# A two-layer AdaLN and FFN kernel: W_dec by two queues and six of eight pieces on VectorE, table rows gathered into W1T's memory, the last FFN's scale and offset on ScalarE, and a new order of steps

## The reference

```
U = (cond_512 @ W_dec + b_dec).reshape(B, 129, 30)      # one matrix for each of 128 sequences
x = x @ (U[:, :-1] @ V) + U[:, -1] @ V                  # layer 0, condition
gate = x @ Wg.T + bg; the two best of 8 experts, softmax of the two
x = x + sum over the two: w * (gelu(x @ W1[e].T + b1[e]) @ W2[e].T + b2[e])
h = ln(ln(x, pw[id], ...), cp[c], ...); t = ln(x, tm[c], ...); s = ln(x, ms[m], ...)
m, n, r = x + three small MLPs of the condition         # rows of the tables by token
x' = ln(silu(concat(w0*h, w1*t, w2*m, w3*n, w4*r, w5*s) @ int_W1 + b) @ int_W2 + b2, int_g, int_be)
f = silu(x' @ w1) * (x' @ w2); f = gelu(f @ h1); f = gelu(f @ h2); x = x + f @ w3    # scaled ternary weights
```

## Time and profile before

| | us |
|---|---|
| median of 3 runs | 456.68 |
| lowest and highest | 456.17, 460.87 |
| the profiled execution | 454.07 |
| its span | 452.2 |

### The profile page before, as it was taken

The page is one execution under the profiler, slowest core; times in us unless marked ns, Lnnn a source line. Parts: engine busy times, 40 slices in busy tenths (PEclk is TensorE's granted clock), DMA queues, the critical chain, the costliest instruction groups (busy, mean ns, idle before and its releaser), DMA issues.

```text
span 452.2 us, 5963 instructions
## 1 busy us (share of the span) xinstructions
PE 425.7 (94%) x1897; PEld 283.9 (63%) x1897; DVE 328.6 (73%) x693; ACT 278.7 (62%) x498; POOL 141.2 (31%) x135
## 2 busy tenths in 40 slices
...
GB/s 235 386 250 93 112 125 256 67 79 204 134 120 144 8 87 227 110 46 13 167 46 46 96 230 6 8 151 166 33 46 77 137 0 2 0 0 25 0 1 50
DMA packets 16847, 45.06 MB, mean 100 GB/s; under 512 B 3209, under 2 KB 5166, under 8 KB 16238
## 3 DMA queue, kind: packets, MB, share of 16 engines
...
...
## 4 chain that ended last, share of the span: by engine, by line
PE 68%; DVE 5%; ACT 4%; issue 2%; POOL 1%; POOLq 0%; ACTq 0%; DVEq 0%
PE bank L737 20%; PE bank L635 18%; PE bank L683 6%; PE bank L777 5%; PE bank L627 5%; PE bank L722 5%; PE bank L690 2%; PE bank L651 2%; PE bank L766 1%; POOL rstd L1421 1%; DVE bn L1163 1%; DVE mG L1153 1%; PE bank L678 1%; PE bank L696 1%; PE bank L646 1%
## 5 line engine op out<-in xcount | busy, mean ns | idle before, releaser
L635 PE MATMUL bank<-mG,W 128*128 128x512 f32 x256 | 120.8, 599 | 0.5 <-DVE mG L1153 0.5
L882 ACT ACTIVATE mG<-bank,keepP 128x512 f32<-128x512 f32 x128 | 85.9, 683 | 33.7 <-PE bank L627 27.0
L1421 POOL TENSOR_TENSOR rstd<-ve,mhalf 128x4 f32<-128x4 f32 x24 | 34.4, 1434 | 177.9 <-DVE ve L1169 177.1
L1153 DVE TENSOR_TENSOR mG<-mG,gwbs 128x1024 f32<-128x1024 f32 x64 | 78.9, 1240 | 1.9 <-DMA gwbs<-gate_w 1.6
L635 PEld LDWEIGHTS bank<-mG,W 128*128 128x128 f32 x256 | 47.5, 192 | 41.3 <-issue 36.8
L627 PE MATMUL bank<-ts,A 96*128 96x512 f32 x128 | 63.8, 533 | 6.8 <-ACT mG L882 5.0
L943 ACT ACTIVATE G<-bank,keepP 128x512 f32<-128x512 f32 x48 | 32.6, 690 | 26.1 <-PE bank L737 25.9
L1401 POOL DMA_INDIRECT gp<-pgb_in,ixall x32 | 39.9, 1247 | 22.4 <-DVE w_l L1069 11.6
L627 PEld LDWEIGHTS bank<-ts,A 96*128 96x128 f32 x128 | 24.0, 191 | 26.7 <-issue 12.6
L737 PE MATMUL bank<-hA_h,h1w_h 128*128 128x512 f32 x96 | 38.8, 404 | 0.0
L737 PE MATMUL bank<-hB_h,h2w_h 128*128 128x512 f32 x96 | 38.8, 404 | 0.0
...
## 6 DMA issues: line engine op xcount, KB each, us to landing
...
W1T<-W1T_in SPq DMA_DIRECT2D x1, 1024.0 KB, 10.0
...
```

The source lines that it names most:

```text
L635: mm = pe.matmul(OACC[:, :], W2[:, e * HC + c, :], mG[n % NMG][:, c, :], start=False, stop=(e == E - 1 and c == HC - 1))
L882: act.activation(mG[e % NMG][:, c % HC, :], HM[n % 2][:, :], ACT.Gelu, bias=b1c[:, c:c + 1]).then_inc(m_gelu, 1)
L1153: dve.tensor_tensor(mG[n % NMG][:, :, :], mG[n % NMG][:, :, :], gwb[(n // 2) % 2][:, n % 2, :].unsqueeze(1).broadcast_to([P, HC, T]), ALU. ...
L1421: step(pool.tensor_tensor(rstd[:, n, :], ve[:, n, :], mhalf[:, :], ALU.pow))
```

## The change

- W_dec comes by two DMAs, rows 0 to 31 from SyncE's queue and 32 to 63 from ScalarE's, ahead of cond_512 and b_dec there. ScalarE issues all its loads before it waits for W_dec, and runs one small activation (`warmA`) that loads its table.
- `PIECES` gives VectorE six pieces of W_dec and ScalarE two (the fourth and the sixth). `WARM` is 5 instead of 6. The products of U still have 65 rows.
- `gap` is 512 columns longer and `ct` lies behind `norms`, so `gp0` lies in W1T's memory and `gap`'s, and the wait for `small_src` goes.
- The splits of the last FFN's weights come in the order h2, w3, h1, w12 instead of w3, w12, h1, h2.
- `ff` is an activation on ScalarE instead of a VectorE instruction.
- The whole `ORDER` is new.

```diff
-        gap = sb("gap", [P, 6144 - KR * (D + 1) - E * H], stack=early)
+        gap = sb("gap", [P, 6656 - KR * (D + 1) - E * H], stack=early)
...
-        WARM = 6
+        WARM = 5
+        PIECES = ("v", "v", "v", "a", "v", "a", "v", "v")
...
             "POOL": (
-                (0, "ix tcl0 tcl1 tcl2 tcl3 srt tcl4 tcl5 tab tcl6 rt0 tcl7 rt1"),
+                (0, "tcl0 tcl1 tcl2 srt tcl3 tcl4 tcl5 ix tab rt0 tcl6 rt1 tcl7"),
...
-            load(Wd[0:MU, :], A["W_dec"], ld_wd)
+            load(Wd[0:MU // 2, :], A["W_dec"][0:MU // 2, :], ld_wd)
...
+            def ff(b):
+                act.wait_ge(yT_mm, b + 1)
+                act.activation(flat(YN), XL[:, :], ACT.Identity, scale=igb[:, 0:1], bias=igb[:, 1:2]).then_inc(f_full, 1)
...
+            load(Wd[MU // 2:MU, :], A["W_dec"][MU // 2:MU, :], ld_wd)
             load(muT[0:MU, :], A["cond_512T"], ld_wd)
             load(Wd[MU:MU + 1, :], A["b_dec"], ld_wd)
+            load(Vk[:, :], A["V"], ld_v)
             load(keepP[:, :], A["keepP"], ld_v)
-            load(Vk[:, :], A["V"], ld_v)
-            act.wait_ge(setup0, 1)
-            act.wait_ge(ld_wd, 48)
             load(earlyP[:, :], A["earlyP"], ld_small)
-            wd = Wd[0:MU + 1, :].rearrange("m (i k) -> m k i", k=KR)
-            for q in range(1, 8, 2):
-                act.activation(Wp[:, 4 * q:min(4 * q + 4, KR), :], wd[:, 4 * q:min(4 * q + 4, KR), :], ACT.Copy).then_inc(wd_odd, 1)
             for b in (1, 2):
                 load(keep[b][:, :], A["xT"][:, b * T:(b + 1) * T], x_in[b])
             load(xTr[0][:, :], A["xT"][:, 3 * T:5 * T], ld_x[0])
             load(w12s[:, :], A["w12T"], ld_w[0])
+            act.wait_ge(setup0, 1)
+            act.activation(warmA[:, :], onesf[:, :], ACT.Copy)
+            act.wait_ge(ld_wd, 64)
+            wd = Wd[0:MU + 1, :].rearrange("m (i k) -> m k i", k=KR)
+            for q in range(8):
+                if PIECES[q] == "a":
+                    mine = slice(4 * q, min(4 * q + 4, KR))
+                    act.activation(Wp[0:MU + 1, mine, :], wd[:, mine, :], ACT.Copy).then_inc(wd_act, 1)
...
-            def ff(b):
-                dve.wait_ge(yT_mm, b + 1)
-                dve.tensor_scalar(flat(YN), XL[:, :], igb[:, 0:1], igb[:, 1:2], ALU.mult, ALU.add).then_inc(f_full, 1)
...
-            dve.wait_ge(ld_wd, 48)
-            for q in range(0, 8, 2):
-                dve.tensor_copy(Wp[:, 4 * q:4 * q + 4, :], wd[:, 4 * q:4 * q + 4, :]).then_inc(wd_even, 1)
+            dve.wait_ge(ld_wd, 64)
+            for q in range(8):
+                if PIECES[q] == "v":
+                    mine = slice(4 * q, min(4 * q + 4, KR))
+                    dve.tensor_copy(Wp[0:MU + 1, mine, :], wd[:, mine, :]).then_inc(wd_dve, 1)
...
-                    pool.wait_ge(small_src, NSMALL)
```

More of the change, by code:

```diff
@@ L137, in build @@
         sa, syT = sz, sth
-        muT = sb("muT", [MU + 1, B], stack=early)
+        muT = sb("muT", [P, B], stack=early)
         Vk = sb("Vk", [KR, P], stack=early)
@@ L160, in build @@
         h1s, h2s = parts(hs, 2048, 2048)
-        Wp = hs[0:MU + 1, 0:KR * (D + 1)].rearrange("m (k i) -> m k i", k=KR)
+        Wp = hs[:, 0:KR * (D + 1)].rearrange("m (k i) -> m k i", k=KR)
+        warmA = sb("warmA", [2, P], stack=early)
         keepB = sb("keepB", [P, 2 * E], stack=early)
@@ L190, in build @@
         xh, tt, ss, hh = [norms[:, i, :, :] for i in range(4)]
-        cs_, ch = [sb(f"c{k}", [P, T]) for k in "sh"]
+        ct, cs_, ch = [sb(f"c{k}", [P, T]) for k in "tsh"]
         TH = sb("TH", [P, T])
@@ L295, in weights_done @@
         def weights_done(eng, *ns):
-            eng.wait_ge(w_lo, max((1, 2, 3, 4)[n] for n in ns))
+            eng.wait_ge(w_lo, max((4, 3, 1, 2)[n] for n in ns))
         def wide(v, n):
@@ L806, in _ @@
             for k in range(KR):
-                if k % 8 == 0:
-                    pe.wait_ge(wd_even, k // 8 + 1)
-                elif k % 8 == 4:
-                    pe.wait_ge(wd_odd, k // 8 + 1)
+                if k % 4 == 0:
+                    who = PIECES[k // 4]
+                    pe.wait_ge(wd_dve if who == "v" else wd_act, PIECES[:k // 4 + 1].count(who))
                 if k == 28:
                     pe.wait_ge(vt_ready, 1)
-                    pe.matmul(bank[7][0:KR, 256:256 + B], Wp[:, :, D], muT[:, :], start=True, stop=True)
+                    pe.matmul(bank[7][0:KR, 256:256 + B], Wp[0:MU + 1, :, D], muT[0:MU + 1, :], start=True, stop=True)
                     pe.wait_ge(ld_small, 16)
@@ L818, in _ @@
                     pe.transpose(bank[7][:, 384:384 + KR], Vk[:, :], ident[0:KR, 0:KR]).then_inc(vt_mm, 1)
-                mm = pe.matmul(bank[k // 4][:, (k % 4) * B:(k % 4 + 1) * B], Wp[:, k, 0:D], muT[:, :], start=True, stop=True)
+                mm = pe.matmul(bank[k // 4][:, (k % 4) * B:(k % 4 + 1) * B], Wp[0:MU + 1, k, 0:D], muT[0:MU + 1, :], start=True, stop=True)
                 if k % 4 == 3 or k == KR - 1:
```

20 lines of the change are left out of this document (11 added, 9 removed), and 115 rows, old and new, of the table ORDER.

## The result

The changed kernel is slower: 467.37 us median of five executions (463.41 to 470.32) against 459.46 of the kernel before on the same chip (456.17 to 460.87). The two medians stand at 1.017; the recorded ratio is 1.0235, with a 95% interval of 1.0189 to 1.0280, which is more than these ten times give. My forecast was 449.8, and its range ended at 456.5.

The account below looks back on a forecast made before the run. TensorE, busy for 94% of the span, was taken as the bound, with time left at start, front and end. -1.9 - 2.5 - 2.5 = -6.9 us took the median from 456.68 to 449.8 us; range 442.0 to 456.5.

Parts of the forecast that it names:

- The load of W_dec: Start: splitting W_dec's load over two queues gains 0 us; at best 1.9 us less, at worst 0.58 us lost.
- Turning W_dec: Start: the wait of 1.07 us for ScalarE goes, seven matmuls of U run fast, U ends at 23.8: -1.9 us.
- my slow bound: Start: if the clock falls as U begins, U ends at 25.0 instead of 25.66 us, -0.7 us.
- the clock stays up: Start rival: two queues load twice as fast or the clock does not fall; -12.9 us in all, 443.8; chance 0.15.
- The first gathers and the root: Front, 41.0 to 124.3 us: block 0's root ahead of a token tile's split removes a TensorE stall; -2.5 us.
- Scale and offset on ScalarE: Last blocks: eight 0.80 us instructions leave VectorE, so block 7's scale no longer waits behind block 5's addition; -2.5 us.
- the slow rival: All blocks: ScalarE's scale delays its Gelus, costing TensorE 1.72 us a block; +6.9 us, 463.6; chance 0.06.

Follow-up runs that it names:

- e3: Kernel after with cond_512 and b_dec loaded ahead of W_dec's half in ScalarE's queue: 468.39 us, 1.0318 of the kernel before.
- e11: Kernel before with six W_dec pieces on VectorE, ScalarE's table loaded early and seven warm-up matmuls instead of six: 449.77 us, 0.9917 of before.
- e7: Kernel before with only the first turn (block 0's, to about 67 us) in the new order: 466.66 us, 1.0235 of before.
- e5: Kernel after with the old start and the first turn in the old order, the rest new: 459.50 us, 1.0024 of the kernel before.
- e6: Kernel before with only ff on ScalarE and block 0's table rows in W1T's memory: 457.47 us, 1.0026 of before.

## Why the prediction was wrong

**The load of W_dec.** "A second queue adds requests only" held: 191 GB/s from 2 to 7 us, no more than the 231 of before (I had said near 231 again). The Trainium skill, "SBUF — State Buffer", section "Door 1: The DMA port swizzle", has it that a half on partitions 0 to 31 and one on 32 to 63 share their ports. The trace agrees: W_dec's last row lands at 6.9 us either way. The step that failed is the next one, "their order against W_dec's last rows on the engines is as it was; I allow the time of one piece's turning, 0.58 us". It cost 1.49 us (9.49 to 10.98), by my reading since W1T no longer stands behind all of W_dec, and e3 shows that the small loads put first don't mend it (11.4).

**Turning W_dec.** The wait for ScalarE did go, and "I let the clock fall at the same 12.2 us" was near (11.4). But U then began at 11.77, behind the fall, so no matmul was fast where I had counted seven. The first token matmul came at 27.43 where I said 24.4; my slow bound, 0.7 us gained, was a loss of 1.0. I had also priced one warm-up matmul less at nothing. e11, with one more and no wait for ScalarE, shows what the start was worth: my rival "the clock stays up" is what the other direction gives, 6.4 us at the first token matmul.

**The low clock behind it.** This is the step that decides, and the sum had no term for it. I let the clock return after U as before (29.2 us in that trace); it returned at 38.7 and was low again from 49 to 66. The sum counted idle time and durations at the clock of before, and took the order between 26 and 67 us as unchanged in effect. In its place the runs show a first turn that alone gives 1.0235 (e7; 9.1 us between the mean times, some 7.0 of them clock not granted).

**The first gathers and the root.** The root did come early, 2.14 us after the statistics (88.39 and 86.25; 5.10 before), and ScalarE's 3.67 us of waiting at block 0's normalisation are gone. But the normalisation itself was no sooner: it began 6.65 us after the statistics (92.90), 6.46 before. So the stall was filled with other steps and not cut from the path. -2.5 us was to be seen as less idle time, and idle time did fall a little (46.8 to 142.1 us: 95.30 - 86.25 = 9.05 instead of 10.5), but what came late ahead of it, in the lists of the first turn, was never costed. I looked at one stall that the new order removes and not at what it puts ahead of the first Gelu and between the products of W1 and V. Both stood in `ORDER`, and both are waits in a strict queue, as the prediction described them for `ff`.

**Scale and offset on ScalarE.** `ff` runs 0.63 us after its turn as forecast, but `fin_h` follows 3.7 us later, behind steps of other blocks on ScalarE. From turn to first FFN matmul are 425.21 - 418.63 = 6.58 us, 6.38 before. The -2.5 us at the end were 0 (e5, with all of the new order behind the first turn: 1.0024; e6: 1.0026), and the hold-up of the slow rival, 1.72 us a block, was 0 too. I gave "slower" 0.06; that the kernel did come out slower was luck for that rival, since its mechanism was not what did it.
